# Node stage of a two-layer graph network: the up product by Strassen's scheme, with a new order of work on four engines

## The reference

```python
h = maximum(layernorm(x), 0)                       # x: 50000 x 256
x = x + segment_sum((h @ W.T)[dst] * edge_weight, src)   # layer 0, 25000 edges, 256 -> 256
h = maximum(layernorm(x), 0)
agg = segment_sum(h[src], dst)                     # layer 1
h = agg + h
h1 = h @ W1 + b1                                   # 256 -> 1024, "up"
h1 = relu((h1 - mean(h1)) * rsqrt(var(h1) + eps) * gamma + beta)   # over the 50000 nodes
x = x + relu(h1 @ W2 + b2)                         # 1024 -> 256, "down"
```

## Time and profile before

| what | value |
|---|---|
| median of three runs | 3862.14 us |
| profiled execution | 3864.24 us, span 3862.4 us |
| TensorE busy | 3422.8 us, 89% |
| VectorE busy | 2277.9 us, 59% |
| ScalarE busy | 2125.0 us, 55% |
| GpSimd busy | 1154.4 us, 30% |
| granted TensorE clock, mean | 0.949 |
| HBM | 173 GB/s over the span |

### The profile page before, as it was taken

How to read it: one execution, slowest core, us unless ns; L and a number is a source line. 1 busy time by engine, 2 the same in 40 slices (tenths; PEclk the granted TensorE clock), 3 DMA queues, 4 the chain that set the end, 5 groups by cost and what they waited for, 6 DMA issues and landing times.

```text
span 3862.4 us, 57303 instructions
## 1 busy us (share of the span) xinstructions
PE 3422.8 (89%) x17113; PEld 2901.6 (75%) x17113; DVE 2277.9 (59%) x5129; ACT 2125.0 (55%) x3435; POOL 1154.4 (30%) x899
## 2 busy tenths in 40 slices
PE   0378887587877879999999999999999999999999
PEld 0367787576666757778888888888888888888888
DVE  0356665576565579955555555555555555555555
ACT  0255555323222279956666666666666666666665
POOL 6667777688888744400000000000000000000000
PEclk9888888789888889999999999999999999999999
DMA  9978876577777799933343343343343343343342
GB/s 344 338 198 191 191 191 140 142 166 163 157 162 156 161 326 378 357 120 109 116 128 109 115 129 109 115 130 109 114 130 109 114 130 109 114 130 109 114 126 68
DMA packets 305856, 619.83 MB, mean 160 GB/s; under 512 B 34998, under 2 KB 186801, under 8 KB 299857
## 3 DMA queue, kind: packets, MB, share of 16 engines
q1 hardware_dynamic: 229440, 515.46, 40.2%
q0 software_dynamic: 75264, 102.81, 15.5%
q10 hardware_dynamic: 1072, 0.76, 0.1%
HBM read 412.83 MB, written 257.28 MB: 173 GB/s over the span
## 4 chain that ended last, share of the span: by engine, by line
PE 64%; POOL 19%; DMA 8%; issue 7%; DVE 1%; ACT 1%; POOLq 0%; SPq 0%; DVEq 0%; ACTq 0%
PE ps_a L1299 28%; PE ps_b L1313 19%; PE ps_b L1314 10%; POOL x_table L553 7%; POOL agg_table L553 7%; DMA x_table<-in_x 4%; POOL edge_tiles L543 4%; PE ps_a L1258 3%; PE ps_a L1260 2%; DMA x_table<-edge_tiles,scatter_now 2%; PE ps_a L1259 2%; DMA agg_table<-edge_tiles,scatter_now 1%; POOL edge_ring L543 1%; DMA edge_tiles<-x_table,gather_ids 0%; ACT edge_tiles L643 0%
## 5 line engine op out<-in xcount | busy, mean ns | idle before, releaser
L1313 PE MATMUL ps_b<-w_hl,late_r 128*128 128x512 f32 x3128 | 1129.0, 396 | 0.0
L1142 DVE TENSOR_TENSOR late_r<-hid,late_r 128x512 fp32r<-128x512 f32 (+1 forms) x784 | 537.2, 685 | 814.8 <-ACT late_r L766 814.8
L761 ACT ACTIVATE hid<-ps_a,bn_bias,bn_scale 128x512 f32<-128x512 f32 (+1 forms) x784 | 609.1, 777 | 734.3 <-PE ps_a L1299 734.3
L1299 PE MATMUL ps_a<-late_r,w_hi 128*128 128x512 f32 x3136 | 983.7, 395 | 0.0
L1314 PE MATMUL ps_b<-w_hl,late_r 128*128 128x256 f32 x3128 | 876.3, 280 | 0.0
L1313 PEld LDWEIGHTS ps_b<-w_hl,late_r 128*128 128x128 f32 x3128 | 587.6, 188 | 138.9 <-issue 0.5
L1299 PEld LDWEIGHTS ps_a<-late_r,w_hi 128*128 128x128 f32 x3136 | 540.2, 188 | 108.8
L1299 PE MATMUL ps_a<-late_r,w_lo 128*128 128x512 f32 x1568 | 611.6, 390 | 0.0
L1314 PEld LDWEIGHTS ps_b<-w_hl,late_r 128*128 128x128 f32 x3128 | 590.0, 189 | 26.4
L766 ACT ACTIVATE late_r<-hid 128x512 fp32r<-128x512 f32 (+1 forms) x784 | 494.8, 631 | 71.7
L1228 PE MATMUL ps_b<-edge_tiles,edge_same 128*128 128x256 f32 x1568 | 405.1, 423 | 0.0
(11 more groups left out here) (123 smaller groups left out, 4407.9 us busy)
## 6 DMA issues: line engine op xcount, KB each, us to landing
x_rows<-x_table SPq DMA_DIRECT2D x291, 512.0 KB, 4.4
late<-agg_table SPq DMA_DIRECT2D x194, 512.0 KB, 5.8
x_table<-in_x SPq DMA_DIRECT2D x10, 5000.0 KB, 32.7
agg_table<-zeros SPq DMA_DIRECT2D x40, 1250.0 KB
hT_table<-h_turned SPq DMA_DIRECT2D x388, 128.0 KB, 2.5
hT_f<-hT_table SPq DMA_DIRECT2D x97, 512.0 KB, 3.6
out<-zeros SPq DMA_DIRECT2D x97, 512.0 KB, 6.7
x_table<-edge_tiles,scatter_now POOLq DMA_INDIRECT x196, 4.1
```

Of the source, the lines that this page charges most:

```text
L761: act.activation(hid[m % 2][:, 0:w].rearrange("p (r a b) -> p r a b", a=BANDS, b=SQUARE), by_row, ACT.Relu, scale=bn_scale[:, m:m + 1], bi ...
L1142: dve.tensor_tensor(hid_lo[m % 4][:, 0:w], hid[m % 2][:, 0:w], hid_hi[m % 4][:, 0:w].bitcast(F32), ALU.subtract).then_inc(hid_lo_ready, 1)
L1299: ins = pe.matmul(ps_a[:, 2 + m % 2, 0:w], w_part[:, kb, cols], h_part[:, kb * w:(kb + 1) * w], start=(t == 0), stop=(t == len(terms) - 1))
L1313: pe.matmul(ps_b[:, r, :], hid_hi[m % 4][:, cols], w2, start=(m == 0), stop=(m == MB - 1), skip_group_check=True)
```

## The change

The up product becomes Strassen's scheme in Winograd's form, on the 2 x 2 blocks of W1 (two contraction blocks of 128, two neighbouring blocks m, called a pair i) and the 2 x 2 blocks of hT (two contraction blocks, two halves of 256 nodes). Seven products stand for eight; each is three matmuls of 256 columns. The weights' sums S1 to S4 are built once on VectorE. The sums T1 to T4 of hT's blocks are built per chunk on GpSimd (`mix_h`) and rounded in high and low parts like hT's own three blocks that are needed. The products are added up in PSUM, in four quarters of two banks per pair: ScalarE copies P1 into the quarter of U2 and P5 to SBUF (`take_p1_p5`), the sixth product accumulates on it, VectorE adds P5 to U2 into one quarter and, after the seventh, P5 to U3 into another; the fourth product of a pair is done one pair later.

`add_agg` and `pick_norm` move from VectorE to GpSimd, VectorE's low parts in the node stage are written by scalar_tensor_tensor (multiply by 1, then subtract), hT has one buffer in fp32 instead of two, and the layout of the output is 32-row bands, so that the output and a second copy of x1 (`x1_out`, loaded for `finish`) move in four DMAs of 1 KB rows each instead of one. The down product is cut into pieces (chunk, m, band) of the same two matmuls as before, dealt out by `ORDER`, in which 5, 1, 62, 73 and 4 are products and each d is one piece; a chunk takes the last 17 pieces of the chunk before and its own first 15.

```diff
+A11, A12, A22, S1, S2, S3, S4 = range(7)
+B11, B22, B21, T1, T2, T3, T4 = range(7)
...
+    def load_x1_out(n, s):
+        for rows, parts, bands in band_rows(x1_table, n):
+            sp.dma_start(x1_out[s % 2][parts, bands, :], rows).then_inc(x1_out_loaded[s % 2], 16)
...
+    def store(n, s, k):
         sp.wait_ge(out_ready, n + 1)
-        if load:
-            load_main(n + LOADS, s)
-        sp.dma_start(chunk_of(out, n), tile_of(out_sb[s % 2], n)).then_inc(out_stored[s % 2], 16)
-        sp.wait_ge(out_stored[s % 2], 16 * turn_of(s, k) + 16)
+        for rows, parts, bands in band_rows(out, n):
+            sp.dma_start(rows, out_sb[s % 2][parts, bands, :]).then_inc(out_stored[s % 2], 16)
+        if has(n, 2):
+            load_x1_out(n + 2, s)
+        if has(n, 5):
+            sp.wait_ge(h_ready, n + 4)
+            load_main(n + 5, s + 5)
+        if has(n, 3):
+            turn_h(n + 3)
+        sp.wait_ge(out_stored[s % 2], 16 * ROWS * turn_of(s, k) + moved_rows(n))
         sp.sem_inc(out_retired, 1)
-    for n in range(LOADS):
...
+    def add_agg(n, s, k):
+        p, j = shape_of(n)
+        pool.wait_ge(ln_ready, n + 1)
+        pool.wait_ge(main_loaded[s % 2], 32 * turn_of(s, k) + 32)
+        if not is_first(n):
+            pool.wait_ge(turned_ready, n)
+        by_square = h[0].rearrange("p j d -> p (j d)").rearrange("p (c j e) -> p j c e", c=CB, e=SQUARE)
+        pool.tensor_tensor(by_square[0:p, 0:j, :, :],
+                           relu_ln[0][0:p, 0:j, :].rearrange("p j (c e) -> p j c e", e=SQUARE),
+                           agg_in[s % 2][0:p, 0:j, :].rearrange("p j (c e) -> p j c e", e=SQUARE), ALU.add).then_inc(h_ready, 1)
+    def mix_h(n):
+        half = width(n) // 2
+        b12, b11, b22, b21 = (hT_f[:, q * half:(q + 1) * half] for q in range(4))
+        t1, t2, t3, t4 = (t_f[:, q * half:(q + 1) * half] for q in range(4))
+        pool.wait_ge(hT_loaded, 16 * n + 16)
+        if not is_first(n):
+            pool.wait_ge(hT_lo_ready, 2 * n)
+        pool.tensor_tensor(t1, b12, b11, ALU.subtract).then_inc(t1_ready, 1)
+        pool.tensor_tensor(t3, b22, b12, ALU.subtract)
+        pool.wait_ge(t1_ready, n + 1)
+        pool.tensor_tensor(t2, b22, t1, ALU.subtract).then_inc(t2_ready, 1)
+        pool.wait_ge(t2_ready, n + 1)
+        pool.tensor_tensor(t4, b21, t2, ALU.subtract).then_inc(t_ready, 1)
+    def main(n, s, k):
+        if has(n, 1):
+            mix_h(n + 1)
+        if has(n, 3):
+            pick_norm(n + 3, (s + 1) % 2)
+        if has(n, 2):
+            add_agg(*after_next(n, s, k))
...
+    pool.wait_ge(gram_used, CHUNKS + 2)
+    add_agg(0, 0, 0)
+    pool.wait_ge(norm_picked, CHUNKS + 2)
+    pick_norm(2, 0)
+    add_agg(1, 1, 0)
+    mix_h(0)
+    main_schedule(pool, main)
...
+    def take_hT(n, s):
+        half = width(n) // 2
+        act.wait_ge(hT_loaded, 16 * n + 16)
+        act.activation(hT_hi[s % 2][:, 0:T1 * half], hT_f[:, half:4 * half], ACT.Copy).then_inc(hT_hi_ready, 1)
+    def take_mixed(n, s):
+        half = width(n) // 2
+        act.wait_ge(t_ready, n + 1)
+        act.activation(hT_hi[s % 2][:, T1 * half:H_PARTS * half], t_f[:, 0:4 * half], ACT.Copy).then_inc(hT_hi_ready, 1)
...
+    def relu_hidden(n, m):
+        w = width(n)
+        i, lower = m // 2, m % 2
+        act.wait_ge(up_done, MB * n + m + 1)
+        if not lower:
+            act.wait_ge(u3_read, PAIRS * n + i + 1)
+        if m >= 2 or not is_first(n):
+            act.wait_ge(hid_lo_ready, MB * n + m - 1)
+        from_ps = quarters(i)[:, 1:3, 0:w // 2] if lower else quarters(i)[:, 0:4:3, 0:w // 2]
+        act.activation(hid[m % 2][:, 0:w].rearrange("p (v x) -> p v x", v=2), from_ps, ACT.Relu,
+                       scale=bn_scale[:, m:m + 1], bias=bn_bias[:, m:m + 1]).then_inc(hid_ready, 1)
+    def hidden_high(n, m):
+        w = width(n)
+        if m >= 4 or not is_first(n):
+            act.wait_ge(down_done, MB * n + m - 3)
+        act.wait_ge(hid_ready, MB * n + m + 1)
+        act.activation(hid_hi[m % 4][:, 0:w], hid[m % 2][:, 0:w], ACT.Copy).then_inc(hid_hi_ready, 1)
+    def take_p1_p5(n, i):
+        half = width(n) // 2
+        act.wait_ge(p1_p5_done, PAIRS * n + i + 1)
+        act.activation(quarters(i)[:, 2, 0:half], quarters(i)[:, 0, 0:half], ACT.Copy)
+        act.activation(p5_sb[i % 2][:, 0:half], quarters(i)[:, 1, 0:half], ACT.Copy).then_inc(p1_p5_taken, 1)
     def main(n, s, k):
+        first = is_first(n)
+        if not first:
+            relu_hidden(n - 1, 6)
+        take_p1_p5(n, 0)
+        if not first:
+            hidden_high(n - 1, 6)
+            relu_hidden(n - 1, 7)
+        if has(n, 2):
+            prepare(*after_next(n, s, k), 0)
+        if not first:
+            hidden_high(n - 1, 7)
+        take_p1_p5(n, 1)
+        relu_hidden(n, 0)
+        hidden_high(n, 0)
+        relu_hidden(n, 1)
+        hidden_high(n, 1)
+        relu_hidden(n, 2)
+        take_p1_p5(n, 2)
+        hidden_high(n, 2)
+        relu_hidden(n, 3)
+        hidden_high(n, 3)
+        if has(n, 2):
+            prepare(*after_next(n, s, k), 1)
+        if has(n, 1):
+            take_hT(n + 1, s + 1)
+        relu_hidden(n, 4)
+        take_p1_p5(n, 3)
+        if has(n, 1):
+            take_mixed(n + 1, s + 1)
+        hidden_high(n, 4)
+        relu_hidden(n, 5)
+        hidden_high(n, 5)
...
+            w1_block = w1_f.rearrange("p k (g h n) -> p k h g n", g=PAIRS, h=2)
+            a11, a21, a12, a22 = (w1_block[:, kb, half, :, :] for kb in range(KB) for half in range(2))
+            s1, s2, s3, s4 = (w1_mixed[:, f, :, :] for f in range(4))
+            chain.then(dve.tensor_tensor(s1, a21, a22, ALU.add))
+            chain.then(dve.tensor_tensor(s3, a11, a21, ALU.subtract))
+            chain.wait()
+            chain.then(dve.tensor_tensor(s2, s1, a11, ALU.subtract))
+            chain.wait()
+            chain.then(dve.tensor_tensor(s4, a12, s2, ALU.subtract))
+            chain.wait()
+            parts = ((A11, a11), (A12, a12), (A22, a22), (S1, s1), (S2, s2), (S3, s3), (S4, s4))
+            for at, part in parts:
+                chain.then(dve.tensor_copy(w1_hi[:, at, :, :], part))
+            chain.wait()
+            for at, part in parts:
+                ins = dve.tensor_tensor(w1_lo[:, at, :, :], part, w1_hi[:, at, :, :].bitcast(F32), ALU.subtract)
+            ins.then_inc(w12_split, 1)
...
+    def hT_low(n, s, mixed):
+        half = width(n) // 2
+        blocks = slice(T1 * half, H_PARTS * half) if mixed else slice(0, T1 * half)
+        whole = t_f[:, 0:4 * half] if mixed else hT_f[:, half:4 * half]
+        dve.wait_ge(hT_hi_ready, 2 * n + (2 if mixed else 1))
+        dve.scalar_tensor_tensor(hT_lo[s % 2][:, blocks], whole, 1.0, hT_hi[s % 2][:, blocks].bitcast(F32),
+                                 ALU.mult, ALU.subtract).then_inc(hT_lo_ready, 1)
...
+    def add_p5_to_u2(n, i):
+        half = width(n) // 2
+        dve.wait_ge(p1_p5_taken, PAIRS * n + i + 1)
+        dve.wait_ge(p6_done, PAIRS * n + i + 1)
+        dve.tensor_tensor(quarters(i)[:, 3, 0:half], quarters(i)[:, 2, 0:half], p5_sb[i % 2][:, 0:half], ALU.add).then_inc(u2_read, 1)
+    def add_p5_to_u3(n, i):
+        half = width(n) // 2
+        dve.wait_ge(up_done, MB * n + 2 * i + 1)
+        dve.tensor_tensor(quarters(i)[:, 1, 0:half], quarters(i)[:, 2, 0:half], p5_sb[i % 2][:, 0:half], ALU.add).then_inc(u3_read, 1)
+    def hidden_low(n, m):
+        w = width(n)
+        dve.wait_ge(hid_hi_ready, MB * n + m + 1)
+        if m >= 4 or not is_first(n):
+            dve.wait_ge(down_done, MB * n + m - 3)
+        dve.scalar_tensor_tensor(hid_lo[m % 4][:, 0:w], hid[m % 2][:, 0:w], 1.0, hid_hi[m % 4][:, 0:w].bitcast(F32),
+                                 ALU.mult, ALU.subtract).then_inc(hid_lo_ready, 1)
...
     def main(n, s, k):
         first = is_first(n)
+        if has(n, 1):
+            turn_squares(n + 1)
+        add_p5_to_u2(n, 0)
+        add_p5_to_u3(n, 0)
         if not first:
+            hidden_low(n - 1, 6)
+            hidden_low(n - 1, 7)
+        add_p5_to_u2(n, 1)
+        hidden_low(n, 0)
+        add_p5_to_u3(n, 1)
+        hidden_low(n, 1)
+        if not first:
+            read_down(n - 1, s - 1, 0)
+        add_p5_to_u2(n, 2)
+        if not first:
+            read_down(n - 1, s - 1, 1)
+        hidden_low(n, 2)
+        add_p5_to_u3(n, 2)
+        if not first:
+            finish(*preceding(n, s, k))
+        hidden_low(n, 3)
+        if has(n, 1):
+            hT_low(n + 1, s + 1, False)
+        add_p5_to_u2(n, 3)
+        hidden_low(n, 4)
+        if has(n, 1):
+            hT_low(n + 1, s + 1, True)
+        add_p5_to_u3(n, 3)
+        hidden_low(n, 5)
...
+    def product(n, s, i, number):
+        weight, part, to, first = {1: (A11, B11, 0, True), 2: (A12, B21, 0, False), 3: (S4, B22, 3, False),
+                                   4: (A22, T4, 2, False), 5: (S1, T1, 1, True), 6: (S2, T2, 2, False),
```

(114 more changed lines are left out.)

274 lines of the change are left out of this document (117 added, 157 removed).

## The result

The changed kernel takes 3899.33 us (median of four runs, 3897.5 to 3902.57) against 3862.09 us; the ratio is 1.0093 with a 95% interval of 1.0081 to 1.0105. The forecast was 3833 us and "faster". The time lies inside the range of 3763 to 3905, but above the 3860 from which on the forecast called itself wrong, and on the other side of no change.

What follows compares the result with a forecast made beforehand. The prediction took TensorE's instruction stream to bound the node stage, at 22.31 us a chunk. From 3864.2 it took 39 for the chunks and added 11 once-only: 3836, stated as 3833 us after the median's offset, range 3763 to 3905.

Steps and rivals of the forecast that it cites:

- Strassen on TensorE: Node stage's up product: 84 short matmuls cost 9.91 us a chunk instead of 11.12, at most 118 us gained.
- The floor: TensorE's least time per node-stage chunk with the change: 21.11 us, 1.21 less than before.
- The port: Node stage, shared SBUF access: GpSimd's add_agg holds VectorE's finish, so TensorE stalls 0.8 us a chunk; period 21.91.
- The hT chain: Node stage, turned h through DRAM and back: hT_f there at 9.4 us, mix_h ready at 13, wanted at 17.0.
- nothing waits for this: Node-stage DMA engines: 3.1 MB a chunk instead of 2.6, under 55% busy, claimed to delay nothing.
- just in time: Chunk's end on VectorE: the last piece of hT's low parts should be done at 21.0 us.
- The once-only costs: Outside the chunk cycle: weights' split 3 us, entering the node stage 5, its end 3; together +11 (0 to 16).
- The lock costs more than Strassen gives: Rival, node stage: add_agg holds VectorE 3.4 us, TensorE stalls 2.0, period 23.1, 3951 us; chance 0.18.
- The PSUM round trips stall too: Rival, node stage: ScalarE's copies cost 0.59 us each, stalls total 1.15 a chunk, 3867 us, no gain; chance 0.14.
- The full gain: Rival, node stage: add_agg and finish don't meet or VectorE has slack; period 21.1 to 21.4, 3763 to 3785; chance 0.23.

Runs made afterwards that it cites:

- experiment 7: Changed kernel with GpSimd's five additions cut to 8 columns each and SP issuing the turned h's stores and load first: 3782.02 us, ratio 0.979 to the kernel before.
- experiment 1: Changed kernel with SP issuing the turned h's stores and load ahead of the loads for chunks to come: 3866.47 us, ratio 1.0007 to the kernel before.
- experiment 5: Changed kernel with the aggregate added on VectorE again, SP's order unchanged: 3796.11 us, ratio 0.9818 to the kernel before.
- experiments 2: Changed kernel with GpSimd adding the aggregate in four operations of 256 columns instead of one of 1024: 3836.6 us, ratio 0.993 to the kernel before.
- version 6: Changed kernel with the aggregate added on VectorE again and SP issuing the turned h first: 3789.24 us, ratio 0.9809 to the kernel before.
- experiment 10: Changed kernel with ScalarE's second half of prepare ahead of pair 2's copies and SP issuing the turned h first: 3845.11 us, ratio 0.9924 to the kernel before.

## Why the prediction was wrong

**Strassen on TensorE: right, 1% too cheap.** Products of 256 columns follow one another in 0.36 us for three, weight loads included. The floor was put at 21.11; experiment 7 measured 21.34. In the changed kernel four triples take 1.43 us (2515.01 to 2516.44), 0.119 a matmul instead of 0.118, and a pair of the down product 0.353 instead of 0.350. The floor's miss is 0.23 x 97.75 = 22 us. What makes the last 1% is open.

**The port: right in mechanism, place and size.** I put GpSimd's hold at 2.2 us and the stall at 0.8, at P5 plus U2 of pair 3. GpSimd's operation is recorded at 2.41, finish grows from 1.2 to 3.20, and experiment 1 has 22.25 - 21.34 = 0.91 a chunk, 11 us more than forecast. The Trainium skill's rule (SBUF — State Buffer, "Who interferes with whom", "The single rule") is borne out by these rows, for scalar_tensor_tensor too. The estimate of 2.25 us that the prediction worked out from the Trainium skill (GPSIMD Engine Reference, "Performance versus the Vector engine") is near the trace's 2.41.

**The hT chain: the step that failed.** The prediction had hT_f there at 9.4, mix_h ready at 13 against 17.0 wanted, and said of the transfers "nothing waits for this". I had taken the 3.94 us of the earlier trace rows for the way through DRAM. That row was measured in a kernel whose last transfer had been issued some 17 us earlier. The change puts the output, x1_out and two loads in front of it, and that alone makes the load of hT start at 5.2 us in the median (experiment 5). My own stall pushes them later: finish ends 2 us late, so its transfers run further into the next turn. In 41 of 93 chunks the load of hT came 6.5 to 7.9 us after the turn. Lateness up to 6.8 us cost almost nothing in experiments 2 and 5. But in the changed kernel GpSimd's long addition of the aggregate moved with it, from finish onto the low parts at the chunk's end, which the prediction had "just in time", and TensorE waited 0.7 to 1.8 us. What the latest chunks would have cost without that addition is not shown. Price: 22.595 - 22.25 = 0.345 a chunk, 34 us. I computed one chunk and asked whether it closes, with every input of the next chunk at its place; I never carried the 2 us into the next one.

The three add up to 22 + 11 + 34 = 67 us, which is the period's miss, (22.595 - 21.91) x 97.75. That the whole miss, 3899 - 3833 = 66, is so near is in part luck: the once-only costs came about 6 us lower than forecast, and the median lies 2 above the profiled execution instead of 3 below it.

**The once-only costs: too high by 6.** The node stage starts at 1672.8 instead of 1672.5, so the longer split of the weights, taken at 3, is hidden. In the changed kernel the stage is 2222.5 us, of which 97.75 x 22.595 = 2208.6 are the chunks: 14 beside them, against 9 before, that is 5 us for entry and end where 8 were forecast. In version 6, which starts its first product at 1674.5, it is 18, against the same 9.

**The rivals.** "The lock costs more than Strassen gives" was to decide from 1.1 us of stall a chunk. The loss came to 22.595 - 21.34 = 1.26, so this rival's side of the threshold won, but with a hold of 2.4 us that meets either finish or the low parts, not with the 3.4 us that it was priced with. "The PSUM round trips stall too" did not happen (experiment 7) and has little slack to spare (experiment 10). "The full gain" (3763 to 3785) is nearly what experiments 5 and 6 reach, once the aggregate is off GpSimd.
